# Two-layer attention block, 16 sequences: score blocks transposed in 64-partition halves, scores in plain float32, first sequence started early, a new order of work

## What is computed

```python
xn = _layernorm(x)
x = x + L0_attn(xn) + L0_ffn(xn)
xn = _layernorm(x)
x = x + L1_attn(xn) + L1_ffn(xn)
```

```python
q, k, v = split(x @ w_qkv)
sim = (q * DH**-0.5) @ k.T + rel * slopes        # masked above the diagonal
out = softmax(sim) @ v
return out @ w_out + b_out
```

## Time and profile before

| | us |
|---|---|
| median of 3 runs | 2792.95 |
| lowest, highest | 2787.28, 2793.64 |
| profiled execution, time | 2788.22 |
| profiled execution, span | 2786.4 |

### The profile page before, as it was taken

The page is one execution under the profiler, slowest core; times in us unless marked ns, Lnnn a source line. Parts: engine busy times, 40 slices in busy tenths (PEclk is TensorE's granted clock), DMA queues, the critical chain, the costliest instruction groups (busy, mean ns, idle before and its releaser), DMA issues.

```text
span 2786.4 us, 49789 instructions
## 1 busy us (share of the span) xinstructions
PE 2554.3 (92%) x16640; PEld 1389.1 (50%) x16640; DVE 1927.8 (69%) x5381; ACT 1962.1 (70%) x4707; POOL 1398.8 (50%) x1353
## 2 busy tenths in 40 slices
PE   3788999999999999999999999999999999999867
PEld 1455555555555545555554555555455555554421
DVE  3336777677777767777776867767676776867664
ACT  2566777777777677787777868777787777778434
POOL 3556455463645546364554636456464645646211
PEclk9899999999999999999999999999999999999976
DMA  2002001020200102020010202002020200202020
GB/s 86 4 1 50 2 17 39 5 50 5 46 5 17 39 6 50 5 47 5 15 41 5 51 1 51 5 10 46 5 50 2 50 5 6 50 2 50 1 50 5
DMA packets 59822, 68.39 MB, mean 25 GB/s; under 512 B 11056, under 2 KB 55344, under 8 KB 56368
## 3 DMA queue, kind: packets, MB, share of 16 engines
q1 hardware_dynamic: 59568, 65.21, 10.3%
HBM read 35.04 MB, written 29.36 MB: 23 GB/s over the span
## 4 chain that ended last, share of the span: by engine, by line
PE 75%; DVE 11%; ACT 5%; issue 5%; POOL 3%; SPq 1%; DMA 0%; DVEq 0%; POOLq 0%; ACTq 0%
PE pj L1304 18%; PE sc L1364 10%; PE pj L1392 10%; PE op L1414 9%; PE sc L1380 9%; PE sc L1458 5%; PE pj L1404 4%; PE pj L1319 4%; PE sc L1451 4%; DVE pq L1072 4%; POOL pq L696 2%; DVE mx L1125 2%; ACT pt L862 2%; PE pj L1296 2%; ACT oraw L846 1%
## 5 line engine op out<-in xcount | busy, mean ns | idle before, releaser
L696 POOL TENSOR_SCALAR pq<-pq,rsum 128x128 f32<-128x128 f32 (+3 forms) x1024 | 1103.0, 1096 | 989.6 <-DVE rsum L1079 989.0
L1125 DVE TENSOR_REDUCE mx<-sc 128x1 f32<-128x512 f32 x1024 | 649.5, 681 | 213.4 <-PE sc L1458 213.2
L862 ACT ACTIVATE pt<-sc 128x512 f32<-128x512 f32 x1024 | 551.3, 601 | 213.0 <-PE sc L1451 210.8
L1072 DVE CUSTOM_DVE_ANT_0 pq<-sc,relkey 128x128 f32<-128x128 f32 (+3 forms) x1024 | 457.1, 483 | 249.2 <-PE sc L1364 242.5
L841 ACT ACTIVATE pt<-sc 128x512 f32<-128x512 f32 x640 | 381.7, 600 | 275.6 <-PE sc L1380 274.1
L827 ACT ACTIVATE pq<-pq,mx 128x128 f32<-128x128 f32 (+3 forms) x1024 | 569.0, 568 | 3.0 <-DVE mx L1072 3.0
L1380 PE MATMUL sc<-ident,pq 128*128 128x128 f32 x2560 | 395.3, 283 | 40.0 <-POOL pq L696 26.9
L1380 PEld LDWEIGHTS sc<-ident,pq 128*128 128x128 f32 x2560 | 288.9, 142 | 222.3 <-issue 130.9
L1392 PE MATMUL pj<-pt,v 128*64 128x512 f32 (+3 forms) x2048 | 303.9, 438 | 14.7 <-DVE KL L1053 13.0
L1414 PE MATMUL op<-pt,v 128*32 128x512 f32 x2048 | 282.6, 626 | 6.4 <-ACT pt L862 6.2
L1304 PE MATMUL pj<-xnT,wqkv 128*128 128x512 f32 x512 | 284.9, 640 | 0.8 <-ACT xnT L772 0.8
(11 more groups left out here) (107 smaller groups left out, 3335.0 us busy)
## 6 DMA issues: line engine op xcount, KB each, us to landing
scr_p<-y SPq DMA_DIRECT2D x160, 128.0 KB, 2.4
QS<-scr_p SPq DMA_DIRECT2D x32, 384.0 KB, 5.8
KS<-scr_p SPq DMA_DIRECT2D x32, 384.0 KB, 8.8
x_in<-in_L_attn_x SPq DMA_DIRECT2D x16, 256.0 KB, 2.9
scr_p<-tanh SPq DMA_DIRECT2D x32, 128.0 KB, 2.4
out_x<-xres SPq DMA_DIRECT2D x16, 256.0 KB, 2.3
QS<-nrow SPq DMA_DIRECT2D x192, 4.0 KB
wqkv<-in_L_attn_w_qkv SPq DMA_DIRECT2D x1, 1536.0 KB, 8.4
```

The costliest lines, as they stand in the source:

```text
L696: pool.tensor_scalar(rows, rows, rsum[:, p % NROWS, c:c + 1], None, ALU.mult).then_inc(s_scl, 1)
L862: act.activation(pt1[:, GS * (m % 2) + 2 * j + h, :], sc[tile_bank("st1", 2 * n + h)][:, :], ACT.Exp, scale=float(DS) ** -0.25).then_inc(s ...
L1072: dve.tensor_tensor_reduce(out=pq[:, at:at + width], in0=sc[tile_bank("mx0", m)][:, left:left + width], in1=relkey[:, T - width:T], scale= ...
L1125: dve.reduce_max(mx1[:, g % 2, at:at + 1], sc[tile_bank("mx1", 2 * t + h)][:, :], AXIS.X).then_inc(s_mxd1, 1)
```

## The change

- Transposes: each 128x128 block is transposed as two halves of 64 partitions, which go to two different `sc` banks (a column block of 64 each). A pair has 3 groups (8, 8 and 4 blocks) with two banks each, and ScalarE makes 6 copies (four of 512, two of 256 columns), each into every other 64 columns of `pt`, where it made 5 of 512.
- Scores: q and k are kept as float32 (`Q0` by ScalarE, `K0` by VectorE, one copy each, each freeing its `pj` bank); one float32 matmul takes the place of the three float32r ones, with its exact width (128 to 512).
- Sums and scaling: the 8 sums of a pair are inverted in 4 steps of 2; GpSimd scales 7 of the 8 row blocks, half of them a step earlier, and VectorE the last (512 columns, `scale_last`).
- Start: x is loaded first, the loads are in three classes with a semaphore each, engines wait only for what a step needs, and the dequantising is spread over ticks 1, 10 and 14 of the first sequence (`prepare`). GpSimd's clearing moves behind its first norm work.
- Order: nearly all constants of ticks and the order in each tick change on every engine.

```diff
@@ constants
-TURNED = (((0, 0),), ((1, 0),), ((0, 1), (0, 3)), ((1, 1), (1, 3)), ((0, 2), (1, 2)))
+TURNED = (((0, 0), (1, 0)), ((0, 1), (0, 3), (1, 1), (1, 3)), ((0, 2), (1, 2)))
-X_AT = -27
-LN0_AT = (-12, -10, -5)
+X_AT = -18
+LN0_AT = (-14, -9, -1)
-STORE_AT = (49, 51)
-STACK_AT = (54, 57)
+STORE_AT = (47, 50)
+STACK_AT = (47, 50)
-STOREOUT_AT = 91
+STOREOUT_AT = 84
-KEY_LAG = 13
+KEY_LAG = 14
...
@@ sync: the first loads
-                for dst, src in loads:
-                    sp.dma_start(dst, src).then_inc(s_ld, 16)
+                sp.dma_start(x_in[:, :, :], x_v[0]).then_inc(s_x, 16)
+                for n in range(3):
+                    for dst, src in loads[n]:
+                        sp.dma_start(dst, src).then_inc(s_ld[n], 16)
@@ scalar
-            def split_q(i, p):
+            def copy_q(i, p):
-                act.activation(QH[:, p % NQ, :], pj[b][:, :], ACT.Copy, scale=qscale[:, p:p + 1]).then_inc(s_spa, 1)
+                act.activation(Q0[:, p % NQ, :], pj[b][:, :], ACT.Copy, scale=qscale[:, p:p + 1]).then_inc(s_pje[b], 1)
-                act.wait_ge(s_tr, i.upto(N_TURN, m + 1))
-                act.activation(pt[:, base:base + T], sc[tile_bank("tr0", m)][:, :], ACT.Copy).then_inc(s_ev, 1)
+                act.wait_ge(s_tr, i.upto(N_TURN, 6 * p + 2 * g + 2))
+                to = pt[:, base + TURN_BASE[g]:base + TURN_BASE[g + 1]].rearrange("p (n h c) -> p n h c", h=2, c=HALF)
+                act.activation(to[:, :, h, :], sc[tile_bank("tr0", m)][:, 0:cols].rearrange("p (n c) -> p n c", c=HALF),
+                               ACT.Copy).then_inc(s_ev, 1)
@@ vector
+            def copy_k(i, p):
+                b, u = pj_use(i, f"k{p}")
+                dve.wait_ge(s_pjf[b], u)
+                dve.tensor_copy(K0[:, p % NQ, :], pj[b][:, :]).then_inc(s_pje[b], 1)
+            def invert_sums(i, p, q):
+                dve.wait_ge(s_exp0, i.upto(L0N, 8 * p + 2 * q + 2))
+                dve.reciprocal(rsum[:, p % NROWS, 2 * q:2 * q + 2], lsum[:, p % NROWS, 2 * q:2 * q + 2]).then_inc(s_rc, 1)
+            def scale_last(i, p):
+                at = PT0 * (2 * (p % NROWS) + 1) + ROW_OFF[NT - 1]
+                dve.wait_ge(s_rc, i.upto(4 * NPAIR, 4 * p + 4))
+                dve.tensor_scalar(pq[:, at:at + T], pq[:, at:at + T], rsum[:, p % NROWS, 7:8], None, ALU.mult).then_inc(s_scv, 1)
@@ tensor
-                    width = max(P * (row + 1), 2 * P)
-                    left = 2 * P if row == 1 else 0
-                    for c, (x, y_) in enumerate(((QH, KH), (QL, KH), (QH, KL))):
-                        for j in range(2):
+                    width = P * (row + 1)
+                    left = P if row == 1 else 0
+                    for j in range(2):
+                        r = slice(HALF * j, HALF * (j + 1))
+                        last = pe.matmul(sc[tile_bank("mx0", m + j)][:, left:left + width], Q0[r, b, P * row:P * (row + 1)],
+                                         K0[r, b, 0:width], start=True, stop=True)
...
-                bank_free(i, "tr0", m)
-                t = sc[tile_bank("tr0", m)]
-                for j, k in TURNED[g]:
-                    for q in range(k, NT):
-                        last = pe.transpose(t[:, to:to + P], pq[:, at:at + P], ident[:, :])
+                for h in range(2):
+                    bank_free(i, "tr0", m + h)
+                blocks = [(j, k, q) for j, k in TURNED[g] for q in range(k, NT)]
+                for n, (j, k, q) in enumerate(blocks):
+                    at = PT0 * (2 * (p % NROWS) + j) + ROW_OFF[q] + P * k
+                    for h in range(2):
+                        r = slice(HALF * h, HALF * (h + 1))
+                        last = pe.transpose(sc[tile_bank("tr0", m + h)][:, HALF * n:HALF * (n + 1)], pq[r, at:at + P], ident[r, r])
```

More of the change, by code:

```diff
@@ L112 @@
 L1_TICKS = 28
[L113 removed]
+FFN1_AT = (56, 56, 57, 59)
 FB_AT = 62
@@ L222, in pj_order @@
             order += misc
+        elif r == 1:
+            second(n, 0)
             order.append(("pv", *pair_at(s, 3)))
-        elif r == 1:
+            order += misc
+            second(n, 1)
+        elif r == 2:
+            second(n, 0)
+            order.append(("v", *pair_at(s, -1)))
+            order += misc
+            second(n, 1)
+        else:
             second(n, 0)
@@ L259, in turned @@
         p, ago = pair_at(s, lag)
-        order.append(("tr0", ago, 5 * p + g))
+        order.extend(("tr0", ago, 6 * p + 2 * g + h) for h in range(2))
     for n in range(TICKS):
@@ L307, in ago, with first @@
         return Seq(self.lo - d, self.j)
+    def first(self):
+        return self.j is None and self.lo == 0
     def live(self):
@@ L574, in load_x @@
             def load_x(i):
-                if i.j is None and i.lo == 0:
-                    sp.dma_start(x_in[:, :, :], x_v[0]).then_inc(s_x, 16)
+                if i.first():
                     return
@@ L730, in body @@
                     s, r = divmod(n, 4)
+                    if b.first() and n == 0:
+                        clear()
                     if r == 0:
@@ L746, in body @@
                             scale_probs(i, p, 2)
+                        small(b, n)
                         p, i = b.pair(s, 1)
@@ L749, in body @@
                             scale_probs(i, p, 3)
+                    elif r == 2:
+                        p, i = b.pair(s, 0)
+                        if i is not None:
+                            scale_probs(i, p, 0)
                         small(b, n)
+                    else:
+                        small(b, n)
+                        p, i = b.pair(s, 0)
+                        if i is not None:
+                            scale_probs(i, p, 1)
             pipeline(pool, body)
@@ L909, in body @@
                     s, r = divmod(n, 4)
+                    if b.first():
+                        prepare(n)
                     if r == 0:
+                        p, i = b.pair(s, -1)
+                        if i is not None:
+                            copy_q(i, p)
                         second_attention(b, n, 0)
@@ L914, in body @@
                             exp0(i, p, 3)
-                        p, i = b.pair(s, -1)
+                        p, i = b.pair(s, 0)
                         if i is not None:
-                            split_k(i, p)
+                            exp0(i, p, 0)
+                        others(b, n)
+                        p, i = b.pair(s, 2)
+                        if i is not None:
+                            copy_turned(i, p, 2)
                         p, i = b.pair(s, 2)
@@ L920, in body @@
                             copy_turned(i, p, 3)
-                        others(b, n)
-                        p, i = b.pair(s, 0)
-                        if i is not None:
-                            exp0(i, p, 0)
-                        second_attention(b, n, 1)
                         p, i = b.pair(s, 2)
@@ L928, in body @@
                             copy_turned(i, p, 4)
+                        second_attention(b, n, 1)
+                    elif r == 1:
+                        p, i = b.pair(s, 2)
+                        if i is not None:
+                            copy_turned(i, p, 5)
+                        second_attention(b, n, 0)
                         p, i = b.pair(s, 3)
@@ L947, in body @@
                         if i is not None:
+                            exp0(i, p, 1)
+                    elif r == 2:
+                        second_attention(b, n, 0)
+                        others(b, n)
+                        p, i = b.pair(s, -1)
+                        if i is not None:
+                            values(i, p)
+                        second_attention(b, n, 1)
+                    else:
+                        p, i = b.pair(s, 0)
+                        if i is not None:
                             exp0(i, p, 2)
-                    else:
                         others(b, n)
+                        second_attention(b, n, 0)
                         p, i = b.pair(s, 1)
@@ L1232, in body @@
                     s, r = divmod(n, 4)
+                    if b.first():
+                        prepare(n)
                     if r == 0:
-                        norms(b, n)
                         others(b, n)
                         second_attention(b, n, 0)
-                        p, i = b.pair(s, -1)
-                        if i is not None:
-                            split_q(i, p)
                         p, i = b.pair(s, 0)
@@ L1273, in body @@
                         second_attention(b, n, 1)
+                        p, i = b.pair(s, 0)
+                        if i is not None:
+                            invert_sums(i, p, 1)
             pipeline(dve, body)
@@ L1527, in body @@
                             project_q(i, p)
-                        p, i = b.pair(s, 2)
-                        if i is not None:
-                            turn_probs(i, p, 2)
                         second_scores(b, n, 0)
```

410 lines of the change are left out of this document (188 added, 222 removed).

## The result

| | before | after |
|---|---|---|
| median us (4 runs each) | 2793.3 | 2725.72 |
| lowest, highest | 2787.28, 2796.29 | 2721.23, 2731.11 |
| profiled execution: time, span | 2788.22, 2786.4 | 2721.23, 2719.4 |

The account below looks back on a forecast made before the run. TensorE's own work was taken as the bound. Span 2786.4 less 107 (14.5 x 7.4 us of period) less 24 at the start gave 2655, plus 1.8 for the time: 2657 us, range 2595 to 2735.

Parts of the forecast that it names:

- Transposes: TensorE's transposes in halves: 0.07 us a block, 1.7 us a pair for 2.8, 1.1 less.
- fourth rival: TensorE's passages between groups vanish where both sides use 64 partitions, no more idle time: 0.3 us a pair, 2610 to 2625; 18%.
- Scores: TensorE's float32 scores in three groups a pair: 0.05 us more than the 2.5 of the kernel before.
- third rival: Float32 scores and transposes on two halves of the rows don't overlap on TensorE: +2.0 us a pair, 2996; 5%.
- the fifth: Rival: a half transpose takes as long as a whole, 0.115 us a block; only the start and little left, 2760; 10%.
- The other engines: Busy us a sequence: ScalarE 119, VectorE 123.6 with 0.8 a pair for `scale_last`, GpSimd 74; none the bound.
- I put the idle time up by 1 us a sequence: TensorE's idle time in the steady state rises by 1 us a sequence, bounds -2.5 and +6.5.
- second rival: Relief goes to waits: `scale_last` heads VectorE's tick, `sc` banks come back later, TensorE stands in `bank_free`: 2715; 17%.
- its own sign: Mark of the second rival: TensorE waits for VectorE over 5 us a sequence more.
- the 7.4 us: Steady period shorter by 7.4 us a sequence: 163.05 - 8.4 of TensorE's work + 1 idle = 155.65.
- The start: Loading x first lets TensorE start at 10 to 12 us: gain 24 us, bounds 15 and 29.
- The factor 14.5: The 7.4 us a period counts 13 times in the steady stretch and 1.5 in filling and tail: 107 us.

Follow-up runs that it names:

- e13: Changed kernel with the second group of transposes ahead of layer 0's first scores of the tick, in the tile order, on TensorE and for ScalarE's copies: 2756.62 us.
- e9: Changed kernel with GpSimd scaling all 8 row blocks of a pair again and VectorE none: 2720.25 us.
- e1: Changed kernel with each 128x128 block transposed whole on 128 partitions again, same groups, tiles, banks, waits and copies: 2758.83 us.
- e14: Changed kernel with the second group of transposes ahead of layer 0's first scores and GpSimd scaling all eight row blocks: 2766.18 us.
- e7: Kernel before with layer 1's row maximum on VectorE over 256 of 512 columns, output not the reference's: 2759.9 us.
- e4: Changed kernel with layer 1's row maximum on VectorE over 256 of 512 columns, output not the reference's: 2685.89 us.
- e11: Changed kernel with the third group of transposes behind layer 1's second chunk of scores, in tile order, and pv0 one step later: 2795.57 us.

## Where the prediction was right and where it was wrong

- **Transposes: right as work, wrong as time.** 1.7 us a pair were forecast; without waits they take 0.61 + 0.61 + 0.40 = 1.6 (13.0 / 8 in e13). In the changed kernel they take 15.9 us a sequence, so 2.0 a pair. The price of now was read too high: 2.8 a pair from two groups, where all groups of the steady stretch make 21.3 / 8 = 2.7. In the trace of after, four records from 1314.68 last 0.34 us and six 0.40, so one more block costs 0.06, the load's distance in the earlier trace rows; whether the load or the half's own stream (0.055 by the prediction's estimate) sets it, no run separates. The 0.025 us that the prediction added for a half by the Trainium skill, TensorEngine Tiling, section Instruction Overhead, does not show here. What the Trainium skill says in the same page's section Key Properties, that changing the tiling mode drains TensorE, agrees with this trace: eight blocks take 0.55 when layer 1's scores, on 51 partitions, follow and 0.64 or more when a 128-partition product does. So the fourth rival's mechanism is real, but only three of a sequence's eight first groups have such a neighbour.

```profile
1314.68 0.34 PE L1423 MATMUL sc<-ident,pq 64*128 64x64 f32 x4
...
1314.68 0.40 PE L1423 MATMUL sc<-ident,pq 64*128 64x64 f32 x6
```

- **Scores: right.** 2.54 against 2.55; float32 on halves of the rows overlaps, so the third rival is out, and with 0.06 a block the fifth too.
- **The other engines: near enough.** ScalarE 118.2 us a sequence (119 forecast), VectorE 119.3 (123.6), GpSimd 78.2 (74). `scale_last` cost VectorE 0.49 and not 0.8: the 0.564 of the earlier trace rows was a mean of 0.33 with GpSimd idle, 0.55 beside its scalings and 1.2 beside its operations on two tensors. The rows of VectorE's new steps:

```profile
L1104 DVE RECIPROCAL rsum<-lsum 128x2 f32<-128x2 f32 x512 | 67.1, 151 | 0.0
L1110 DVE TENSOR_SCALAR pq<-pq,rsum 128x512 f32<-128x512 f32 x128 | 62.3, 486 | 4.5
```

- **The step that failed: "I put the idle time up by 1 us a sequence".** It rose by 4.9, and busy time fell by 5.3, not 8.4. I had costed the order of TensorE as a list of works with one gap each, and had not laid the new tile order on the five banks. Had I done it, the trace of the kernel before would have given the wait: the sixth tile in a row needs both of VectorE's reads of the scores, and only the eight blocks of the second group, 0.55 to 0.65 us, lie between. These reads, of 128 and 256 columns, were there to be read:

```profile
L1072 DVE CUSTOM_DVE_ANT_0 pq<-sc,relkey 128x256 f32<-128x256 f32 x256 | 107.5, 420 | 0.7 <-issue 0.5
L1072 DVE DVE_READ_ACCUMULATOR2_ANT mx<- 128x1 f32 x1024 | 84.6, 83 | 0.3
L1072 DVE CUSTOM_DVE_ANT_0 pq<-sc,relkey 128x128 f32<-128x128 f32 x256 | 70.2, 274 | 42.0 <-PE sc L1364 39.4
```

  0.27 + 0.42 us and the read of the last maximum are about 0.7, and they start some 0.3 after the scores' end. The second rival had the mechanism (the relief goes to `bank_free`, 2715, 17%) and came within 11 us, but named `scale_last` as its cause, which e9 rules out; its own sign, over 5 us a sequence more of waiting for VectorE, was not reached either (3.6).
- **Where the 7.4 us went.** Summed over the 13 steady periods of each trace, a matmul's cost being the distance to the next one's start, in us a sequence:

| TensorE's work | before | e1 (whole blocks) | after |
|---|---|---|---|
| transposes | 21.3 | 19.3 | 15.9 |
| layer 0's scores | 19.8 | 20.8 | 20.2 |
| layer 1's scores (both kinds) | 26.8 | 28.8 | 28.9 |
| all else | 95.2 | 96.1 | 97.7 |

  The transposes give 5.4 of the 8.8 that were forecast, for 3.7 of it went into the wait inside the twelve blocks. Of the 5.4, 5.0 are lost at other steps: 0.5 at the scores (0.4 forecast), 2.1 at layer 1's scores, 2.5 at the rest. With whole blocks such losses are there too, 1.0, 2.0 and 0.9. They come with the new order, waits at each step included; which of its many moves makes which wasn't tried.
- **The start: right**, 20.5 at the first `xb` sum for 24 (bounds 15 and 29).
- **The factor 14.5: wrong, in the other direction.** I gave filling and tail 1.5 periods' share, 11 us; they gave 26.1 and 15.7. Whole blocks lose only 1.9 of the filling's and 5.9 of the tail's. TensorE waited 19.8 us for GpSimd between the first two sums before and 1.2 after, and the clock was 0.93 there before and 1.00 after. These are shown, and e9 and e14 show that the row block that VectorE scales is a part of it: given back to GpSimd it makes this stretch 2.8 us longer in one order of TensorE (0.2 by the third sum) and 9.0 in the other (8.1), where the clock falls to 0.93 too. e13's order alone makes it 7 longer. That the inversion in four steps, which lets GpSimd begin before the last sum, makes the rest wasn't tried. The tail's 15.7 stays open as well; its clock was 0.85 before and 0.89 after, and VectorE's work counts there (17 us a sequence less took 22.6 us off the tail before, e7, and 7.9 after, e4). The two errors cancelled in part: with filling and tail at the 11 us of the forecast, the time would have been 2757, outside of the stated range. That the time fell inside it is luck.

## What to carry to other kernels

When several producers take turns on few buffers, lay the new order on the buffers and count what stands between a tile and the one that reuses its bank, before you sum the work: work that is saved between the two turns into waiting if the reader is not faster too. Test where an engine's time counts by leaving work out at a place without a hand-over: if the period follows, the engine is the bound, and the lost gain is in the order. And judge a start or filling by its own dependencies; it can give more than the steady state.

## What the hardware showed that was not expected

- Float32 transposes on two halves of the partitions ran side by side at 0.062 us a block for 0.11 whole, as close as two weight loads stood in the earlier trace rows (0.06).
- The granted clock did not follow the mean busy share: 93% busy went with 1.00 in one order and with 0.97 in another (e11), in which single waits of TensorE for VectorE lasted up to 2.8 us; 92% went with 1.00 in e13, whose waits lasted up to 1.5. What in the order takes the clock down wasn't tried.
- VectorE's scaling of 128x512 took 0.485 to 0.489 us each time, with a scaling of GpSimd always beside it, and it was GpSimd that paid: its scalings of 384 columns took 1.54 us in the mean beside `scale_last` and 1.26 otherwise (1.25 in e9, where VectorE has none). That is 2.3 us a sequence of the 4 by which GpSimd was over the forecast. The 0.06 above the 0.426 of the earlier trace rows can't be put down to GpSimd: that is another instruction, and it took 0.426 beside a scaling too, in the one case of the changed kernel.
